# Who takes Sinkhorn's reciprocals: a power of -1 on GpSimd instead of a reciprocal on VectorE

## The chip, the cores and the metric

The kernel runs on one core of a Trainium2 chip. The metric is the device time of one execution in microseconds (us). The core has TensorE (PE) for matmuls, VectorE (DVE), ScalarE (ACT) and GpSimd (POOL) for everything elementwise, and SyncE (SP), which here only starts DMAs. Each engine takes its own instructions in the order in which they are written, and engines wait for each other by counting semaphores.

## The reference, cut to what matters

The input is x of shape 8 x 512 x 2048. A gated cross attention over windows of 128 columns comes first, and then a gated mixing block, which holds the loop that this case is about:

```python
x = x + jnp.tanh(g_xattn[0]) * xattn(_layernorm(x), ctx_4096, ...)
x = x + jnp.tanh(g_ffn[0]) * ffn(_layernorm(x), ...)

# inside ffn: 4 x 4 logits for each of the 8 * 512 rows
def sinkhorn_log(logits, num_iters=50, tau=0.1):
    Z = logits / tau
    def step(carry, _):
        u, v = carry
        u = -jax.nn.logsumexp(Z + v[..., None, :], axis=-1)
        v = -jax.nn.logsumexp(Z + u[..., :, None], axis=-2)
        return ((u, v), None)
    (u, v), _ = jax.lax.scan(step, (u0, v0), None, length=num_iters)
    return jnp.exp(Z + u[..., :, None] + v[..., None, :])
...
x_mixed = jnp.einsum('btij,btjc->btic', H_res, x_streams)   # H_res from sinkhorn_log
```

## The kernel before, in words

Partitions hold 128 of the 512 rows at a time, so one batch element is four row tiles (DT = 4). Attention is done in 32 chunks of 512 columns (4 for each batch element), each chunk in 8 units. All engines loop over the same counter `g`: one step of `g` is one unit of attention, plus whatever the tables at the top of the program place at that step for other chunks and for the mixing block of the batch element before. 32 steps are one batch element. There is no planner: the order on each engine is the order of the calls in its loop over `g`.

The kernel does Sinkhorn's iterations in the linear domain. For each batch element `ke` is [128, 4 tiles, 4, 4], 64 numbers in a partition. The first of the 50 iterations is done with logarithms, and so is a return to them after iteration 25 (`return_scales`); the other 49 iterations are done as 98 half iterations. A half iteration multiplies `ke` by the scales of the other side, sums rows or columns (16 sums in a partition) and inverts the sums:

- GpSimd, `scale` (L522 to L526): `kp = ke * sa` or `kp = ke * sv`, 128x64. It waits for `scale_made` and counts `kp_made`. In 96 of the 98 halves there is such a product (`SCALED`); two halves for each batch element sum `ke` itself.
- VectorE, `half_iteration` (L1125 to L1141): a `tensor_reduce` of `kp` into `ssum` (L1134, 128x16), and behind it, by way of a wait on its own semaphore (`cf.link`), a `reciprocal` of `ssum` into `sa` or `sv` (L1135), which counts `scale_made`.

The halves of one batch element are a chain: no half starts before the one in front of it. `SINK` puts two iterations, four halves, into a step: 12 steps, the step with iteration 25 alone, a step for the logarithms, and 12 steps again. `half_at(f, its, 0)` to `half_at(f, its, 3)` in VectorE's loop stand between the attention's maximum (L1002), the reads of projections (L982, L1019) and `divide` (L1010), the sums of the mixing block's output (`add_stream` L1179, `add_y` L1192, `make_xpre` L1167) and the statistics (L968, L1043). `scale_at(f, its, 0)` to `scale_at(f, its, 3)` in GpSimd's loop stand between its other work, which the tables place once for each of four row tiles in 8 steps: `norm_x` (L454) behind the first, `split_ctx` (L465) behind the second, `split_x` (L460) behind the third. Behind the fourth come GpSimd's own DMAs, `add_x` (L474) and `store` (L480), four in 8 steps.

After iteration 25, VectorE holds until the scales are there and then asks ScalarE for their logarithms (L1137, L1138). After iteration 50 it holds in the same way and makes the mixing coefficients (`coefficients`, L1148 to L1161).

## Time and profile before

| | us |
|---|---|
| median of 3 runs | 1913.92 |
| lowest and highest | 1908.95, 1915.57 |
| the profiled execution's own time | 1919.96 |
| its span, first to last instruction | 1918.2 |

| engine | busy us | share of the span | instructions |
|---|---|---|---|
| PE (matmul) | 1418.2 | 74% | 12448 |
| DVE | 1434.5 | 75% | 3684 |
| ACT | 942.4 | 49% | 1889 |
| POOL | 868.2 | 45% | 1461 |

The shares are means over a span with three kinds of stretches: about 340 us at the start without any Sinkhorn, some 1250 us in which attention of one batch element and the mixing block of the one before run side by side, and the last 300 us, in which only the mixing block is left and TensorE is mostly idle. How full an engine is where the change acts has to be read from a stretch, not from this table.

### The profile page before, as it was taken

The page shows a single profiled execution, that of the slowest core. Times are in us where ns is not written, and L with a number is a line of the kernel's source. Part 1 is how long each engine was busy: PE and PEld are TensorE (multiplying, and loading weights), DVE is VectorE, ACT ScalarE, POOL GpSimd, SP SyncE. Part 2 cuts the span into 40 slices and gives each one's busy share as a digit, 9 for nine tenths or more (in the row PEclk, how much of TensorE's full clock was granted, in tenths as well). Part 3 has the DMA queues.
Part 4 walks back from the last instruction along what each step waited for, and adds up shares of the span by engine and source line. Part 5 has one row for each costly group of instructions (what it writes and reads, how often), then busy time and mean ns, then how long its engine had stood idle before and what let it go on. Part 6 is the DMA issues. An engine that isn't in the chain of part 4 may idle for free. (4 is left out here: it accounts for less than half of the span.)

```text
span 1918.2 us, 35465 instructions
## 1 busy us (share of the span) xinstructions
PE 1418.2 (74%) x12448; PEld 857.5 (45%) x12448; DVE 1434.5 (75%) x3684; ACT 942.4 (49%) x1889; POOL 868.2 (45%) x1461
## 2 busy tenths in 40 slices
PE   2778899888888888888888888888888976421223
PEld 1545555544554455455544454445544554210111
DVE  3344445666688888888888888888888888777787
ACT  2445565555465556555655555554555554210112
POOL 4433333445445554555455645555565523323310
PEclk9889998999899999998999989998999986755656
DMA  7556655565566666666666656666555543321132
GB/s 247 150 152 198 177 159 150 156 165 152 151 177 189 188 189 176 176 184 167 183 192 188 184 170 177 185 173 168 167 168 168 144 119 92 88 77 44 55 101 107
DMA packets 173984, 299.79 MB, mean 156 GB/s; under 512 B 23664, under 2 KB 74736, under 8 KB 169712
## 3 DMA queue, kind: packets, MB, share of 16 engines
q1 hardware_dynamic: 147184, 230.41, 39.3%
q0 software_dynamic: 26624, 67.12, 15.2%
q8 instruction: 100, 1.64, 0.3%
q14 instruction: 76, 0.62, 0.1%
HBM read 179.75 MB, written 67.11 MB: 129 GB/s over the span
## 5 line engine op out<-in xcount | busy, mean ns | idle before, releaser
L526 POOL TENSOR_TENSOR kp<-ke,sv 128x64 f32<-128x64 f32 x376 | 186.5, 496 | 254.7 <-DVE sv L1135 245.0
L1134 DVE TENSOR_REDUCE ssum<-kp 128x16 f32<-128x64 f32 x768 | 181.9, 237 | 147.3 <-POOL kp L526 142.3
L604 PE MATMUL pr<-x_hl,wq 128*128 128x512 bf16 x768 | 234.1, 470 | 67.4 <-POOL x_hl L460 67.4
L526 POOL TENSOR_TENSOR kp<-ke,sa 128x64 f32<-128x64 f32 x392 | 126.7, 323 | 347.1 <-DVE sa L1135 347.1
L805 ACT ACTIVATE probs<-st_ps,key_bias 128x512 f32<-128x512 f32 x256 | 174.3, 681 | 184.1 <-PE st_ps L702 182.8
L1002 DVE TENSOR_REDUCE negm<-s_ps 128x4 bf16<-128x512 f32 x256 | 167.9, 656 | 111.9 <-PE s_ps L688 103.7
L631 PE MATMUL pr<-o_sb,wo 128*128 128x512 bf16 x768 | 186.2, 389 | 49.1 <-DVE o_sb L1026 38.1
L460 POOL TENSOR_TENSOR x_hl<-xc,x_hl 128x512 bf16<-128x512 f32 x128 | 172.6, 1349 | 103.4 <-ACT x_hl L773 103.4
L618 PE MATMUL pr<-wv,ctx_hl 128*128 128x256 bf16 x1536 | 193.1, 286 | 6.4 <-POOL ctx_hl L465 6.4
L465 POOL TENSOR_TENSOR ctx_hl<-ctx_raw,ctx_hl 128x512 bf16<-128x512 f32 x128 | 151.2, 1182 | 71.1 <-ACT ctx_hl L767 71.0
L604 PE MATMUL pr<-x_hl,wk 128*128 128x512 bf16 x768 | 176.4, 379 | 0.0
L604 PEld LDWEIGHTS pr<-x_hl,wq 128*128 128x128 bf16 x768 | 88.3, 118 | 193.1 <-issue 112.5
L651 PE MATMUL pr<-id_sb,x1c 128*128 128x128 f32 x512 | 89.9, 315 | 113.2 <-DMA x1c<-in_dram 113.2
L618 PEld LDWEIGHTS pr<-wv,ctx_hl 128*128 128x128 bf16 x1536 | 153.4, 103 | 40.7 <-issue 17.8
L700 PE MATMUL st_ps<-q_st,k_st 96*128 96x128 bf16 x1024 | 149.0, 222 | 17.9 <-ACT probs L805 14.8
L1010 DVE TENSOR_TENSOR o_sb<-av_ps,rden 128x128 f32<-128x128 f32 x256 | 70.5, 276 | 109.1 <-ACT rden L814 108.9
L787 ACT ACTIVATE q_hl<-pr,bq_sb 128x512 bf16<-128x512 f32 x64 | 44.0, 687 | 217.1 <-PE pr L604 217.1
L702 PE MATMUL st_ps<-id_bf,negm 128*128 128x128 bf16 x1024 | 148.4, 222 | 0.0
L675 PE MATMUL pr<-id_sb,xpre 128*128 128x128 f32 x128 | 24.5, 325 | 161.9 <-DVE xpre L1167 161.9
L631 PEld LDWEIGHTS pr<-o_sb,wo 128*128 128x128 bf16 x768 | 69.3, 99 | 167.4 <-issue 67.0
L728 PE MATMUL f<-wb,xpt 128*128 128x512 f32 x256 | 134.3, 674 | 8.5 <-ACT xpt L884 8.5
L1179 DVE SCALAR_TENSOR_TENSOR otile<-x1t_even,cmat,otile 128x512 f32<-128x512 f32 x192 | 136.0, 749 | 0.3
(140 smaller groups left out, 3106.8 us busy)
## 6 DMA issues: line engine op xcount, KB each, us to landing
xs<-in_dram SPq DMA_DIRECT2D x128, 256.0 KB, 3.8
xc<-in_dram SPq DMA_DIRECT2D x32, 1024.0 KB, 5.6
ctx_raw<-in_dram SPq DMA_DIRECT2D x32, 1024.0 KB, 5.2
x1c<-in_dram POOLq DMA_DIRECT2D x64, 512.0 KB, 6.0
x_dram<-x1c SPq DMA_DIRECT2D x32, 1024.0 KB, 5.4
out_dram<-otile POOLq DMA_DIRECT2D x64, 512.0 KB, 3.8
q_st<-q_hl SPq DMA_DIRECT2D x384, 64.0 KB
k_st<-k_hl SPq DMA_DIRECT2D x384, 64.0 KB
```

The lines of the kernel that those rows point to most:

```text
L460: nc.gpsimd.tensor_tensor(x_hl[:, G % 2, 1, t, :], xc[:, t, :], x_hl[:, G % 2, 0, t, :], ALU.subtract).then_inc(x_split, 1)
L465: ins = nc.gpsimd.tensor_tensor(ctx_hl[:, 1, t, :], ctx_raw[:, t, :], ctx_hl[:, 0, t, :], ALU.subtract)
L526: nc.gpsimd.tensor_tensor(kp[:], ke[:], v, ALU.mult).then_inc(kp_made, 1)
L604: ins = nc.tensor.matmul(bank(what)[:], w[:, a, t, i * P:(i + 1) * P], x_hl[:, G % 2, m, t, :], start=(t == 0 and a + m == 0), stop=(t == ...
L618: ins = nc.tensor.matmul(bank(what)[:, j * E:(j + 1) * E], ctx_hl[:, a, t, win], wv[:, m, t, :], start=(t == 0 and a + m == 0), stop=(t == ...
L631: ins = nc.tensor.matmul(bank(what)[:], wo[:, a, et, t * P:(t + 1) * P], o_part(G, et, m), start=(et == 0 and a + m == 0), stop=(et == ET ...
L700: nc.tensor.matmul(part, k_st[0:ROWS, G % 2, et, h, win], q_st[0:ROWS, G % 2, et, h, win], start=True, stop=False)
L702: ins = nc.tensor.matmul(part, negm[:, k % 2, h:h + 1].broadcast_to([P, P]), id_bf[:], start=False, stop=True)
L805: nc.scalar.activation(probs[:, k % 2, :], st_ps[:], ACT.Exp, bias=key_bias[:, b % 2, w:w + 1], scale=SCALE).then_inc(exp_done, 1)
L1002: nc.vector.tensor_reduce(negm[:, k % 2, :], s_ps[:].rearrange("p (h j) -> p h j", h=HPT), AX.X, ALU.max, negate=True).then_inc(max_done, 1)
L1134: cf.link(nc.vector.tensor_reduce(s_t, k, AX.X, ALU.add))
L1179: ins = nc.vector.scalar_tensor_tensor(out=otile[:, i, :], in0=x1[:, j * C:(j + 1) * C], scalar=cmat[:, f % 2, t, i, j:j + 1], in1=otile[: ...
```

## The change: GpSimd inverts the sums

A new function `invert` on GpSimd raises the 16 sums of each partition to the power of -1. It is a `tensor_tensor` with a tile `minus` that holds -1.0 everywhere. `scale` calls it in front of the product that needs its result. Two inversions have no product behind them (after iteration 25 and after iteration 50); `invert_last` does these, behind `scale_at(f, its, 3)`. VectorE keeps the sum and drops the reciprocal and the wait on its own semaphore. `sum_made` is the new semaphore from VectorE to GpSimd; `scale_made` is now counted by GpSimd; GpSimd's products and VectorE's waits at those two halves wait for it.

```diff
@@ -212,6 +212,7 @@
         gt = sb("gt", [P, 8])
         ones = sb("ones", [P, P])
         spare = sb("spare", [P, 1])
+        minus = sb("minus", [P, DT * N])
         csum = sb("csum", [P, NL])
         bn_a = sb("bn_a", [P, DT, 4, 6])
         mv_a = sb("mv_a", [P, DT, 2])
@@ -310,6 +311,7 @@
         x1_added = [sem(f"x1_added{i}") for i in range(2)]
         x1_stored = sem("x1_stored")
         x1t_loaded = [sem(f"x1t_loaded{i}") for i in range(2)]
+        sum_made = sem("sum_made")
         scale_made = sem("scale_made")
         kp_made = sem("kp_made")
         bias_ready = sem("bias_ready")
@@ -519,8 +521,15 @@
                     newton(r[:, 5, :], r[:, 2, :], r[:, 4, :], r[:, 1, :])
                     nc.gpsimd.tensor_tensor(r[:, 5, :], r[:, 5, :], r[:, 3, :], ALU.mult).then_inc(rb_ready, 1)
 
+            def invert(f, it, half):
+                n = HALVES * f + 2 * (it - 1) + half
+                pool.wait_ge(sum_made, n + 1)
+                dst = (sv if half else sa)[:].rearrange("p t i -> p (t i)")
+                nc.gpsimd.tensor_tensor(dst, ssum[:], minus[:], ALU.pow).then_inc(scale_made, 1)
+
             def scale(f, it, half):
 
+                invert(f, it if half else it - 1, 1 - half)
                 pool.wait_ge(scale_made, HALVES * f + 2 * (it - 1) + half)
                 v = bcast(sa[:], 3, N) if half else bcast(sv[:], 2, N)
                 nc.gpsimd.tensor_tensor(kp[:], ke[:], v, ALU.mult).then_inc(kp_made, 1)
@@ -530,8 +539,15 @@
                 if (it, half) in SCALED:
                     scale(f, it, half)
 
+            def invert_last(f, its):
+                if its[0] == RETURN:
+                    invert(f, RETURN, 1)
+                elif its[1] == ITERS - 1:
+                    invert(f, ITERS - 1, 1)
+
             pool.memset(q_st[ROWS:ROWS + 1], 1.0).then_inc(zeroed, 1)
             pool.wait_ge(zeroed, 1)
+            pool.memset(minus[:], -1.0)
             variance(0)
             xstat(0)
             for g in range(FIRST, LAST):
@@ -555,6 +571,7 @@
                 for H, t in at_step(g, -2, LOW_X_AT):
                     split_x(H, t)
                 scale_at(f, its, 3)
+                invert_last(f, its)
                 if 0 <= G - 1 < NG and r in (6, 7):
                     add_x(G - 1, r - 6)
                 for done, t in tiles_at(g, 4):
@@ -1131,8 +1148,7 @@
                     k = ke[:]
                 if half:
                     k = k.rearrange("p t i j -> p t j i")
-                cf.link(nc.vector.tensor_reduce(s_t, k, AX.X, ALU.add))
-                nc.vector.reciprocal((sv if half else sa)[:], s_t).then_inc(scale_made, 1)
+                nc.vector.tensor_reduce(s_t, k, AX.X, ALU.add).then_inc(sum_made, 1)
                 if half and it == RETURN:
                     dve.wait_ge(scale_made, HALVES * f + 2 * it)
                     ask(nc.vector.memset(spare[:, 0:1], 0.0))
```

GpSimd in program order, around the end of iteration 25 of the first batch element; `scale_made` before is counted by VectorE. Before:

```order
L526 TENSOR_TENSOR kp<-ke,sv 128x64 [waits scale_made]
L526 TENSOR_TENSOR kp<-ke,sa 128x64 [waits scale_made]
L465 TENSOR_TENSOR ctx_hl<-ctx_raw,ctx_hl 128x512 [waits ctx_hi]
L454 TENSOR_SCALAR xc<-xc,ra 128x512 [waits xstat_ready,xc_loaded]
L465 TENSOR_TENSOR ctx_hl<-ctx_raw,ctx_hl 128x512 [waits ctx_hi]
```

And the same place of the changed kernel (its lines 528, 535, 467 and 456 are `invert`, `scale`, `split_ctx` and `norm_x`):

```order
L528 TENSOR_TENSOR sv<-ssum,minus 128x16 [waits sum_made]
L535 TENSOR_TENSOR kp<-ke,sv 128x64 [waits scale_made]
L528 TENSOR_TENSOR sa<-ssum,minus 128x16 [waits sum_made]
L535 TENSOR_TENSOR kp<-ke,sa 128x64 [waits scale_made]
L467 TENSOR_TENSOR ctx_hl<-ctx_raw,ctx_hl 128x512 [waits ctx_hi]
L528 TENSOR_TENSOR sv<-ssum,minus 128x16 [waits sum_made]
L456 TENSOR_SCALAR xc<-xc,ra 128x512 [waits xstat_ready,xc_loaded]
```

Each product now has an inversion right in front of it, and the last inversion of iteration 25 stands behind the subtraction that splits the context.

VectorE in program order at the same place, before:

```order
L1134 TENSOR_REDUCE ssum<-kp 128x16 [waits kp_made]
L1135 RECIPROCAL sv<-ssum 128x16 [waits dve_ffn]
L1002 TENSOR_REDUCE negm<-s_ps 128x4 [waits st_full,s_full]
L1134 TENSOR_REDUCE ssum<-kp 128x16 [waits kp_made]
L1135 RECIPROCAL sa<-ssum 128x16 [waits dve_ffn]
L982 SCALAR_TENSOR_TENSOR q_hl<-pr,bq_sb,q_hl 128x512 [waits qk_hi]
L1010 TENSOR_TENSOR o_sb<-av_ps,rden 128x128 [waits rden_done]
L1134 TENSOR_REDUCE ssum<-kp 128x16 [waits kp_made]
L1135 RECIPROCAL sv<-ssum 128x16 [waits dve_ffn]
L1138 MEMSET spare 128x1 [waits scale_made]
L1002 TENSOR_REDUCE negm<-s_ps 128x4 [waits st_full,s_full]
```

And of the changed kernel (its lines 1151, 1154, 1019, 999 and 1027 are the sum, the request to ScalarE, the maximum, a read of a projection and `divide`):

```order
L1151 TENSOR_REDUCE ssum<-kp 128x16 [waits kp_made]
L1019 TENSOR_REDUCE negm<-s_ps 128x4 [waits st_full,s_full]
L1151 TENSOR_REDUCE ssum<-kp 128x16 [waits kp_made]
L999 SCALAR_TENSOR_TENSOR q_hl<-pr,bq_sb,q_hl 128x512 [waits qk_hi]
L1027 TENSOR_TENSOR o_sb<-av_ps,rden 128x128 [waits rden_done]
L1151 TENSOR_REDUCE ssum<-kp 128x16 [waits kp_made]
L1154 MEMSET spare 128x1 [waits scale_made]
L1019 TENSOR_REDUCE negm<-s_ps 128x4 [waits st_full,s_full]
```

The reciprocals are gone from VectorE and nothing else there changes place. Its wait at L1154 is now one for GpSimd.

## Rows read from the trace of the kernel before

**Rows 1.** The page: the chain that ended last, its shares by engine

```profile
DVE 7%; POOL 1%; DMA 1%; issue 1%; PE 0%; ACT 0%; DVEq 0%; ACTq 0%
```

**Rows 2.** Busy us of each engine by stretch (start:end, length, then engines)

```profile
1039.90:1089.90 50.00, 41.02 (x380) 24.48 (x380) 44.68 (x119) 30.15 (x60) 29.39 (x50) 0.95 0.63 186
1744.00:1918.00 174.00, 44.81 (x77) 18.89 (x75) 129.62 (x294) 27.36 (x41) 35.92 (x89) 0.60 0.23 82
```

**Rows 3.** Waits: who waited for whom, us in total, times, longest

```profile
POOL kp L526 <- DVE sa L1135: 347.1, 269, 9.9
POOL kp L526 <- DVE sv L1135: 245.0, 273, 2.6
...
DVE ssum L1134 <- POOL kp L526: 142.3, 293, 1.9
```

**Rows 4.** Groups by line: busy us, mean ns of one, idle before

```profile
L1134 DVE TENSOR_REDUCE ssum<-kp 128x16 f32<-128x64 f32 x768 | 181.9, 237 | 147.3 <-POOL kp L526 142.3
...
L1135 DVE RECIPROCAL sa<-ssum 128x16 f32<-128x16 f32 x392 | 99.2, 253 | 13.4
L1135 DVE RECIPROCAL sv<-ssum 128x16 f32<-128x16 f32 x392 | 99.2, 253 | 13.4
```

**Rows 5.** The same view: GpSimd's products and its other instructions

```profile
L526 POOL TENSOR_TENSOR kp<-ke,sv 128x64 f32<-128x64 f32 x376 | 186.5, 496 | 254.7 <-DVE sv L1135 245.0 <-ACT x_hl L773 8.4
L460 POOL TENSOR_TENSOR x_hl<-xc,x_hl 128x512 bf16<-128x512 f32 x128 | 172.6, 1349 | 103.4 <-ACT x_hl L773 103.4
L526 POOL TENSOR_TENSOR kp<-ke,sa 128x64 f32<-128x64 f32 x392 | 126.7, 323 | 347.1 <-DVE sa L1135 347.1
L487 POOL TENSOR_TENSOR rb<-rb 128x4 f32<-128x4 f32 x16 | 3.2, 203 | 1.3
```

**Rows 6.** GpSimd in order of time, last batch element: start, us, instruction, idle before

```profile
1749.35 0.30 POOL L526 TENSOR_TENSOR kp<-ke,sv 128x64 f32<-128x64 f32 x1 [0.66 <-DVE sv L1135]
1750.27 0.30 POOL L526 TENSOR_TENSOR kp<-ke,sa 128x64 f32<-128x64 f32 x1 [0.62 <-DVE sa L1135]
```

**Rows 7.** VectorE over the same moments

```profile
1749.69 0.22 DVE L1134 TENSOR_REDUCE ssum<-kp 128x16 f32<-128x64 f32 x1 [0.41 <-POOL kp L526]
1749.94 0.25 DVE L1135 RECIPROCAL sa<-ssum 128x16 f32<-128x16 f32 x1
1750.60 0.26 DVE L1134 TENSOR_REDUCE ssum<-kp 128x16 f32<-128x64 f32 x1 [0.41 <-POOL kp L526]
```

**Rows 8.** GpSimd in order of time: a chain of its own; a DMA between products

```profile
1057.06 1.25 POOL L474 DMA_DIRECT2D x1c<-in_dram  x1
1057.88 0.77 POOL L526 TENSOR_TENSOR kp<-ke,sv 128x64 f32<-128x64 f32 x1
...
1103.39 0.20 POOL L487 TENSOR_TENSOR rb<-rb 128x4 f32<-128x4 f32 x1
1103.68 0.20 POOL L488 TENSOR_SCALAR rb<-rb 128x4 f32<-128x4 f32 x1
```

**Rows 9.** Both engines where iteration 25 ends

```profile
1021.82 1.16 POOL L465 TENSOR_TENSOR ctx_hl<-ctx_raw,ctx_hl 128x512 bf16<-128x512 f32 x1
...
1022.18 0.25 DVE L1134 TENSOR_REDUCE ssum<-kp 128x16 f32<-128x64 f32 x1
1022.46 0.25 DVE L1135 RECIPROCAL sv<-ssum 128x16 f32<-128x16 f32 x1
```

**Rows 10.** VectorE in order of time: two of the 32 stretches between sums

```profile
1048.48 1.36 DVE L1179 SCALAR_TENSOR_TENSOR otile<-x1t_even,cmat,otile 128x512 f32<-128x512 f32 x2
1049.88 0.22 DVE L1134 TENSOR_REDUCE ssum<-kp 128x16 f32<-128x64 f32 x1
1050.13 0.25 DVE L1135 RECIPROCAL sa<-ssum 128x16 f32<-128x16 f32 x1
1051.15 0.27 DVE L1134 TENSOR_REDUCE ssum<-kp 128x16 f32<-128x64 f32 x1 [0.77 <-POOL kp L526]
```

## The prediction, made before the changed kernel ran

> **What bounds the kernel now.** I read the chain that ended last first, and put it aside: its shares add up to about a tenth of the span [rows 1], so it says little of the stretches in which the change acts. Next the busy time by stretch. Between 1039.9 and 1089.9 us stand exactly 8 steps with four half iterations each, 32 halves in 50 us, 6.25 us a step. VectorE is busy for 44.7 of these 50 us, TensorE for 41.0, GpSimd for 29.4 [rows 2]. VectorE is the fullest, and GpSimd has 20.6 us to spare.
>
> Then the waits, to see whether that spare time is free. It is not all free: GpSimd waits 592 us in total for the two reciprocals, and VectorE waits 142 us for GpSimd's product [rows 3]. The halves are one chain that goes to and fro between the two engines. Where VectorE has nothing else to do between two halves, the chain turns as fast as it can: a product every 0.92 to 0.96 us, of which GpSimd works 0.30 and sits idle 0.62 to 0.66 [rows 6], while VectorE sums for 0.22 to 0.26, inverts for 0.25 and then waits 0.41 [rows 7]. Where VectorE has other work between two halves, that work covers GpSimd's part: behind the 1.36 us of L1179 the sum starts at once, without a wait [rows 10]. So a step is VectorE's own work plus a few bare turns of the chain, and what counts on GpSimd is how much longer its part of a half may get before that cover is gone.
>
> **What the change removes.** 784 reciprocals of 0.253 us on VectorE, 198 us [rows 4], or 8.1 us of each 50, with some 0.03 us of a wait on its own semaphore at each. Nothing else of VectorE moves.
>
> **What it adds.** 784 powers of 16 elements on GpSimd, P us each, and one more handoff inside GpSimd, from the power to the product. That handoff is a wait on its own semaphore. Its price is in the trace: chained GpSimd instructions of 0.20 us stand 0.29 us apart, so 0.09 us [rows 8]. The handoffs from VectorE to GpSimd and back stay as they were. A memset of 16 elements at the start is nothing beside the wait for the first statistics. The power also reads two operands in SBUF like the product does, so the slower products that show up in the mean (0.496 us for those from sv, 0.323 for those from sa, [rows 5]) may change places with it; I leave their sum alone.
>
> **The price P.** No instruction before is a power. From below it can hardly be less than the product of the same form: that takes 0.203 us for 4 elements and 0.30 us for 64 [rows 5, 6], so 0.0016 us an element over 0.197, and 0.22 us for 16. [...] Taking 30 to 50 such steps (my assumption, no row shows it) and for each the 0.0016 us an element of a small product gives 16 x 30 x 0.0016 + 0.2 = 1.0 us to 16 x 50 x 0.0016 + 0.2 = 1.5 us. With the 0.0023 us an element of the large subtractions ((1.349 - 0.2) / 512, [rows 5]) 50 steps are 2.0 us. I take 1.0 us, the lower figure of the nearer row, because a step inside one instruction has no load and store of its own; the ends that I keep are 0.22 and 2.0.
>
> The Trainium skill has no price for a power. Its "GPSIMD Engine Reference", section "Performance pitfalls for Q7 kernels", says that a chain of dependent fp32 operations costs 4 cycles an element for each link, and its table puts the engine at 1.2 GHz. No run here shows it yet. By it 30 links over 16 elements would be 1.6 us and 0.2 over, 1.8 us, an estimate from that page; that is the second rival below.
>
> **The sum.** With P near 1 us the cover is gone and GpSimd sets the pace, so I count its 8 steps. Its busy time is 29.4 us [rows 2], less 0.9 us, since two of the DMAs that it issues in 8 steps are shown as 1.25 us while the next product starts 0.82 us after them [rows 8]: 28.5 us. Behind 16 of the 32 products stand other instructions in its order (the four each of L454, L465 and L460, and four DMAs), so that VectorE's sum is done beside them; there only the handoff of 0.09 us is idle, 1.4 us. Behind the other 16 it waits for the sum: the idle 0.64 us of a bare turn [rows 6], less the reciprocal and its wait (0.25 and 0.03), plus the handoff of 0.09, is 0.45 us, 7.2 us in all. 28.5 + 1.4 + 7.2 = 37.1, so 8 steps take 37 + 32 P us, as long as that is clearly over what VectorE needs. For P = 1.0 this is 69 us where there were 50, and a step is 8.6 us. VectorE's work without the reciprocals, 36.6 us, fits into that; only the few stretches of over 1.5 us between two sums make GpSimd wait, which I leave out with about 1 us.
>
> There are 784 / 32 = 24.5 such groups of 32 halves in the program: 24.5 x 19 = 466 us. The last batch element, in which TensorE is nearly idle [rows 2], runs the same chain (rows 6 are from there) and loses as much. At the end of iteration 25 VectorE now holds the whole queue behind L1154 until GpSimd has finished the subtraction in front of the last power. That subtraction runs from 1021.8 to 1023.0, and the sum is ready at 1022.4 [rows 9]: 0.6 us more beside the power itself, and at iteration 50 nothing more than the power. What is queued there are the attention's maximum and the read of a projection, for which TensorE and ScalarE wait. 8 x 0.6 and the two handoffs are some 8 us. Together 1918 + 466 + 8 = 2392 us of span, 2394 of execution. The profiled execution was 1919.96, 6 us over the median of 1913.92, so for a median I say **2390 us**. In general the time is about 1608 + 784 P for P over 0.4.
>
> **Rival 1: the power is as cheap as a product, and the change is faster.** For it speaks that VectorE is the fullest engine and loses 8.1 of its 44.7 us. With P = 0.22 the bare turn stays what it was: 0.25 + 0.03 leave, 0.22 + 0.09 come. Of 32 stretches between sums, 18 have over 0.8 us of other work on VectorE and can be shorter by 0.28 us each, 5 us in 50; where GpSimd's own 1.2 to 1.6 us stand in front of the power (12 of 32) the power is late and takes about half of that back. That leaves 2.5 to 5 us in 50, or 60 to 120 us: 1800 to 1855 us. This is the other side, and it decides at P of about 0.33 us, where the two effects meet. [...]
>
> **Rival 2: GpSimd computes the power link by link.** P = 1.4 to 2.0 us, by the larger of the figures above. At 1.8 us it is 1608 + 1411 = 3020 us. [...]
>
> **Rival 3: the power costs about twice the reciprocal.** The Trainium skill says in "GPSIMD Engine Reference", section "Engine selection", that elementwise work is about half as fast here as on VectorE. From rows, twice 0.253 us is P = 0.5: 37 + 16 = 53 us for 8 steps plus about 1 us in which VectorE is late, 24.5 x 4 = 98 us more, or about 2010 us. Rows 4 and 5 put a small product on GpSimd (0.22) level with a small operation on VectorE, so the rule is weak for small tiles.
>
> **Rival 4: nothing to see.** P between 0.30 and 0.36 us, gains and losses equal, 1908 to 1920.
>
> **How the numbers follow.** 2390 us, with P between 0.7 and 1.4 and so 2150 to 2700: chance 0.40. Rival 2, 2700 to 3180: 0.22. Rival 3, P from 0.36 to 0.7, 1920 to 2150: 0.19. Rival 1, under 1908: 0.12. Rival 4: 0.04. The last 0.03 are for a power that is not computed in the engine's vector form at all and takes ten times as long. This measurement can tell a change from none at about 0.3%, 6 us. Slower by more: 0.40 + 0.22 + 0.19 + 0.03 = 0.84; within: 0.04; faster: 0.12. The range that holds 8 in 10 must reach to both sides, since the price is open by a factor of nine: 1850 to 3100 leaves out the better half of rival 1 and the upper end of rival 2, about 0.2.
>
> **What would show it.** In the profile after, the group of L528 gives P directly, and the rest hangs on it. If I am right, its mean is near 1 us, GpSimd is the fullest engine with about 80% of the span (868 + 784 = 1652 us), 8 steps take 69 us, VectorE's waits at L1151 for L535 grow from 142 to over 500 us, and all of VectorE's, ScalarE's and TensorE's busy times stay as they were apart from the reciprocals. TensorE will wait more and its granted clock may fall below the 0.95 of these steps [rows 2]; that would lengthen its work, but not the end, as long as GpSimd sets the pace. The sum is wrong if 8 steps do not take 37 + 32 P with the measured P. The direction is wrong if P is under 0.33 us.

## The result: twice the time, far outside the range

| | median us | lowest to highest | executions |
|---|---|---|---|
| before | 1911.85 | 1908.95 to 1915.57 | 4 |
| after | 3855.24 | 3854.09 to 3859.77 | 4 |

The ratio is 2.0145, with a 95% interval of 2.0091 to 2.0199. The forecast was 2390 us and the range ended at 3100 us. The direction was right and the size was not. The page of the changed kernel begins with the engines' busy time; the second line below is the share of the chain that ended last, the third the granted clock in 40 slices, in tenths.

```profile
PE 1727.5 (45%) x12293; PEld 1015.1 (26%) x12448; DVE 1330.7 (35%) x2900; ACT 962.6 (25%) x1889; POOL 3135.6 (81%) x2246
...
POOL 8%; DVE 2%; issue 1%; DMA 1%; PE 0%; ACT 0%; DVEq 0%; ACTq 0%
...
PEclk9998666766777666686668666676667655555556
```

GpSimd went from 868 to 3136 us and is now the fullest engine. VectorE's busy time fell by 104 us, not by the 198 us of its reciprocals; ScalarE's rose by 20. TensorE's is 309 us longer for the same matmuls, since its granted clock is lower: 0.691 as a mean where it was 0.876 (1.0 is its upper level of 2.4 GHz, 0.5 the lower one of 1.2 GHz). This is a consequence of the waiting: TensorE is busy for 45% of the span, and VectorE's wait for its scores (L1019, L1002 before) even fell, from 103.7 to 79.6 us. The groups answer to [rows 4, 5], with busy us, mean ns of one, then the idle time before and who ended it:

```profile
L528 POOL TENSOR_TENSOR sv<-ssum,minus 128x16 f32<-128x16 f32 x392 | 1224.3, 3123 | 90.0 <-DVE ssum L1151 88.9
L528 POOL TENSOR_TENSOR sa<-ssum,minus 128x16 f32<-128x16 f32 x392 | 1148.5, 2930 | 151.6 <-DVE ssum L1151 151.6
L1151 DVE TENSOR_REDUCE ssum<-kp 128x16 f32<-128x64 f32 x768 | 186.1, 242 | 2232.6 <-POOL kp L535 2232.6
...
L535 POOL TENSOR_TENSOR kp<-ke,sa 128x64 f32<-128x64 f32 x392 | 117.3, 299 | 30.7
L535 POOL TENSOR_TENSOR kp<-ke,sv 128x64 f32<-128x64 f32 x376 | 112.4, 299 | 29.5
...
L1195 DVE SCALAR_TENSOR_TENSOR otile<-x1t_even,cmat,otile 128x512 f32<-128x512 f32 x192 | 156.8, 857 | 0.3
```

The power takes 3.03 us as a mean over its 784. With that alone GpSimd has 2373 us more to do. VectorE's wait for the product, which answers to the last line of [rows 3], went from 142 to 2233 us. The products, read in [rows 5] as 496 and 323 ns, are now all 299 ns. The last row is part of the answer to VectorE's missing gain: this group, L1179 before, took 136.0 us with 749 ns each, and takes 857 now. Two instructions of the chain in order of time, first on GpSimd and then on VectorE, show what [rows 6, 7] showed of before:

```profile
2001.00 2.90 POOL L528 TENSOR_TENSOR sv<-ssum,minus 128x16 f32<-128x16 f32 x1 [0.44 <-DVE ssum L1151]
2003.98 0.30 POOL L535 TENSOR_TENSOR kp<-ke,sv 128x64 f32<-128x64 f32 x1
2004.26 0.77 POOL L456 TENSOR_SCALAR xc<-xc,ra 128x512 f32<-128x512 f32 x1
2005.00 2.90 POOL L528 TENSOR_TENSOR sa<-ssum,minus 128x16 f32<-128x16 f32 x1
```

```profile
2000.66 0.26 DVE L1151 TENSOR_REDUCE ssum<-kp 128x16 f32<-128x64 f32 x1 [2.27 <-POOL kp L535]
2000.84 0.68 DVE L1019 TENSOR_REDUCE negm<-s_ps 128x4 bf16<-128x512 f32 x1
2004.31 0.22 DVE L1151 TENSOR_REDUCE ssum<-kp 128x16 f32<-128x64 f32 x1 [2.79 <-POOL kp L535]
```

GpSimd goes from the power to the product 0.08 us later; where another instruction of its own stands behind the product, the next power needs no wait at all. VectorE does its 0.68 us of other work and then stands for 2.79 us. A half turns in 3.65 us here, where a bare one (with no other work on either engine) took 0.92. The stretch of 8 steps answers to the first line of [rows 2], with the columns as there:

```profile
1723.50:1853.80 130.30, 57.27 (x375) 32.88 (x380) 42.08 (x86) 29.82 (x55) 121.48 (x81) 0.68 0.25 71
```

It took 50.0 us and takes 130.3. GpSimd is busy for 121.5 of them and idle for 8.8. ScalarE's 29.8 us are nearly the 30.2 of before.

### The profile page after: what moved, and what is told of

Its sections match the earlier page's. It is cut to its first block and busy times, and to the rows that moved or that the text cites. A ratio compares the mean times of both kernels' runs of the same rounds, so it can differ in the third digit from the quotient of the medians.

```text
span 3852.6 us, 35310 instructions
## 1 busy us (share of the span) xinstructions
PE 1727.5 (45%) x12293; PEld 1015.1 (26%) x12448; DVE 1330.7 (35%) x2900; ACT 962.6 (25%) x1889; POOL 3135.6 (81%) x2246
## 5 line engine op out<-in xcount | busy, mean ns | idle before, releaser
L528 POOL TENSOR_TENSOR sv<-ssum,minus 128x16 f32<-128x16 f32 x392 | 1224.3, 3123 | 90.0 <-DVE ssum L1151 88.9
L528 POOL TENSOR_TENSOR sa<-ssum,minus 128x16 f32<-128x16 f32 x392 | 1148.5, 2930 | 151.6 <-DVE ssum L1151 151.6
L705 PE MATMUL s_ps<-k_st,q_st 97*128 97x128 bf16 x1024 | 127.2, 262 | 641.1 <-DVE negm L1019 629.4
L648 PE MATMUL pr<-o_sb,wo 128*128 128x512 bf16 x706 | 248.5, 499 | 350.1 <-DVE x1c L1036 140.3
L732 PE MATMUL av_ps<-probs,v_t 128*32 128x128 f32 x2048 | 137.9, 350 | 335.8 <-DVE o_sb L1027 335.6
L705 PEld LDWEIGHTS s_ps<-k_st,q_st 97*128 97x128 bf16 x1024 | 87.2, 116 | 732.4 <-DVE negm L1019 484.3
L635 PE MATMUL pr<-wv,ctx_hl 128*128 128x256 bf16 x1536 | 232.2, 322 | 7.1 <-POOL ctx_hl L467 6.9
L621 PE MATMUL pr<-x_hl,wk 128*128 128x512 bf16 x736 | 206.6, 439 | 4.3 <-issue 2.9
L1019 DVE TENSOR_REDUCE negm<-s_ps 128x4 bf16<-128x512 f32 x256 | 174.3, 681 | 84.3 <-PE s_ps L705 79.6
L717 PE MATMUL st_ps<-q_st,k_st 96*128 96x128 bf16 x1024 | 192.4, 264 | 16.9 <-DVE negm L1019 9.4
L719 PE MATMUL st_ps<-id_bf,negm 128*128 128x128 bf16 x1024 | 191.8, 263 | 0.0
L1195 DVE SCALAR_TENSOR_TENSOR otile<-x1t_even,cmat,otile 128x512 f32<-128x512 f32 x192 | 156.8, 857 | 0.3
```

The source lines that it names most:

```text
L528: nc.gpsimd.tensor_tensor(dst, ssum[:], minus[:], ALU.pow).then_inc(scale_made, 1)
L621: ins = nc.tensor.matmul(bank(what)[:], w[:, a, t, i * P:(i + 1) * P], x_hl[:, G % 2, m, t, :], start=(t == 0 and a + m == 0), stop=(t == ...
L635: ins = nc.tensor.matmul(bank(what)[:, j * E:(j + 1) * E], ctx_hl[:, a, t, win], wv[:, m, t, :], start=(t == 0 and a + m == 0), stop=(t == ...
L648: ins = nc.tensor.matmul(bank(what)[:], wo[:, a, et, t * P:(t + 1) * P], o_part(G, et, m), start=(et == 0 and a + m == 0), stop=(et == ET ...
L705: ins = nc.tensor.matmul(s_ps[:, h * W:(h + 1) * W], q_st[0:ROWS + 1, G % 2, et, h, win], k_st[0:ROWS + 1, G % 2, et, h, win], start=True, ...
L717: nc.tensor.matmul(part, k_st[0:ROWS, G % 2, et, h, win], q_st[0:ROWS, G % 2, et, h, win], start=True, stop=False)
```

## The experiments

Eleven kernels, in three groups; the kernel before ran beside each group, with medians of 1913.66, 1912.88 and 1912.17 us. Two questions were open. Why does the power cost 2.9 us, and does the sum hold with its real price? And would the change have been faster had the power been cheap, as Rival 1 said?

### probe: powers by themselves

The kernel before, with a chain of GpSimd instructions ahead of its loop, on tiles that nothing else uses.

```diff
+            cp.link(nc.gpsimd.tensor_tensor(po[:, 0:16], pb[:, 0:16], pe_[:, 0:16], ALU.mult))
+            cp.link(nc.gpsimd.tensor_tensor(po[:, 0:1], pb[:, 0:1], pe_[:, 0:1], ALU.pow))
+            ... (0:4, 0:16, 0:64, 16 partitions x 16, then exponents 2 and -0.5 and a base of 1, at 0:16)
```

> The kernel before, with a row of GpSimd instructions of its own ahead of the loop, each waiting for the one before, on tiles that nothing else uses: one product of 128x16, powers of -1 of 128x1, 128x4, 128x16, 128x64 and 16x16 (16 partitions), powers of 2 and of -0.5 of 128x16 with base 2.7, and a power of -0.5 with base 1. The time stays within 10 us of the kernel before. Theory A (the power has this price by itself, element by element): 128x16 takes 2.90 us here too, where VectorE does nothing with two operands, and 128x1, x4 and x64 take 0.37, 0.87 and 11.0 us (0.2 and 0.169 an element); 16 partitions cost what 128 do. Theory C (the power is slow only beside VectorE, which shares memory access with GpSimd): 128x16 takes about 1 us here. A price that depends on exponent or base would show in the last three.

The single execution took 1926.2 us, 12.5 more than before, a little over the 10 that were expected for the delayed start. GpSimd in order of time (L541 is a product, L542 to L546 are powers of -1, L548 has the exponent 2, the last row below a base of 1):

```profile
8.15 0.21 POOL L541 TENSOR_TENSOR pout<-pbase,pexp 128x16 f32<-128x16 f32 x1
8.44 0.58 POOL L542 TENSOR_TENSOR pout<-pbase,pexp 128x1 f32<-128x1 f32 x1
9.10 1.02 POOL L543 TENSOR_TENSOR pout<-pbase,pexp 128x4 f32<-128x4 f32 x1
10.20 2.90 POOL L544 TENSOR_TENSOR pout<-pbase,pexp 128x16 f32<-128x16 f32 x1
13.18 10.55 POOL L545 TENSOR_TENSOR pout<-pbase,pexp 128x64 f32<-128x64 f32 x1
23.80 2.89 POOL L546 TENSOR_TENSOR pout<-pbase,pexp 16x16 f32<-16x16 f32 x1
...
26.98 2.90 POOL L548 TENSOR_TENSOR pout<-pbase,pexp 128x16 f32<-128x16 f32 x1
...
33.36 2.90 POOL L552 TENSOR_TENSOR pout<-pbase,pexp 128x16 f32<-128x16 f32 x1
```

From 16 to 64 elements the price rises by 7.65 us for 48 elements, 0.159 us an element; 2.90 less 16 x 0.159 leaves 0.36 us, and the rows of 1 and 4 elements put the fixed part at 0.42 to 0.38. The exponents, the two bases and the number of partitions change nothing. So the price belongs to the operation and its length, not to its place in the kernel, and Theory C falls: VectorE is idle beside the last row. A product of the same form is 0.21 us.

### cheap: the same instruction as a product

The power becomes a product of ones with ones, so the sums aren't inverted and the scales are 1. Instructions, operand shapes and waits stay.

```diff
-                nc.gpsimd.tensor_tensor(dst, ssum[:], minus[:], ALU.pow).then_inc(scale_made, 1)
+                nc.gpsimd.tensor_tensor(dst, minus[:], minus[:], ALU.mult).then_inc(scale_made, 1)
```

> The changed kernel with a product of two constant tiles of ones (128x16) in the place of each power, so the reciprocal is left out and every scale is 1; waits and order are those of the change. Theory A (the price P alone decides): P is 0.22 us, and by rival 1 of the prediction the kernel is faster than before, 1800 to 1855 us, 8 steps in 45 to 47.5 us. Theory B (the inversion costs by where it stands: one more handoff in the chain and the place behind GpSimd's other work): no gain, 1905 us or more.

1925.83 us (1920.46 to 1928.44), ratio 1.0057 [1.0041, 1.0073]: 0.6% slower than before, though VectorE's busy time is 1305.3 us instead of 1434.5. The bare turn is as long as it was (0.92 to 0.96 us between these powers' stand-ins, L528):

```profile
1751.05 0.21 POOL L528 TENSOR_TENSOR sv<-minus 128x16 f32<-128x16 f32 x1 [0.38 <-DVE ssum L1151]
1751.97 0.21 POOL L528 TENSOR_TENSOR sa<-minus 128x16 f32<-128x16 f32 x1 [0.33 <-DVE ssum L1151]
1752.93 0.65 POOL L528 TENSOR_TENSOR sv<-minus 128x16 f32<-128x16 f32 x1 [0.37 <-DVE ssum L1151]
```

The third row is the other finding: the same instruction takes 0.65 us when VectorE runs an operation with two operands in SBUF beside it. Between 400 and 1900 us, 133 stand-ins run beside L1195, which reads two tiles in SBUF, and their median is 0.65 us; 84 run beside the maximum L1019, which reads PSUM, and take 0.21. VectorE and GpSimd over one stretch between two sums:

```profile
980.82 0.27 DVE L1151 TENSOR_REDUCE ssum<-kp 128x16 f32<-128x64 f32 x1 [0.23 <-POOL kp L535]
981.01 2.11 DVE L1195 SCALAR_TENSOR_TENSOR otile<-x1t_even,cmat,otile 128x512 f32<-128x512 f32 x2
983.38 0.22 DVE L1151 TENSOR_REDUCE ssum<-kp 128x16 f32<-128x64 f32 x1 [0.26 <-POOL kp L535]
...
981.87 0.66 POOL L528 TENSOR_TENSOR sv<-minus 128x16 f32<-128x16 f32 x1
...
982.61 0.67 POOL L535 TENSOR_TENSOR kp<-ke,sv 128x64 f32<-128x64 f32 x1
```

From sum to sum this is 2.56 us. The same stretch of the kernel before takes 2.16 us, with the reciprocal in it:

```profile
978.11 0.25 DVE L1134 TENSOR_REDUCE ssum<-kp 128x16 f32<-128x64 f32 x1
978.39 0.25 DVE L1135 RECIPROCAL sv<-ssum 128x16 f32<-128x16 f32 x1
978.56 1.67 DVE L1179 SCALAR_TENSOR_TENSOR otile<-x1t_even,cmat,otile 128x512 f32<-128x512 f32 x2
980.27 0.22 DVE L1134 TENSOR_REDUCE ssum<-kp 128x16 f32<-128x64 f32 x1
```

Rival 1 falls as it was priced: with an instruction that takes its 0.22 us alone there is no gain. In its place it takes 0.43 us for sv and 0.24 for sa as a mean. VectorE's wait for the product is 309.7 us in total where it was 142.3 [rows 3].

### four: a power of 4 of the 16 elements

The other 12 scales are set to 1 once.

```diff
-                nc.gpsimd.tensor_tensor(dst, ssum[:], minus[:], ALU.pow).then_inc(scale_made, 1)
+                nc.gpsimd.tensor_tensor(dst[:, 0:4], ssum[:, 0:4], minus[:, 0:4], ALU.pow).then_inc(scale_made, 1)
```

> The changed kernel with powers of 4 of the 16 sums (128x4); the other 12 scales stay 1, so three quarters of the inversions are left out. Theory A: P about 0.87 us, 1608 + 784 x 0.87 = 2290 us. If the power has a large fixed part (call, table, setup) and a small one for each element, P stays near 2.5 us and the time over 3400.

2391.86 us in a single execution. The power took 1.13 us as a mean (1.229 for sv, 1.035 for sa), not the expected 0.87, and 8 steps took 70.5 us:

```profile
1409.71:1480.25 70.54, 48.70 (x382) 27.25 (x381) 41.92 (x87) 29.11 (x55) 61.30 (x81) 0.83 0.45 131
```

By chance its time is the forecast one: the prediction's own formula says 1608 + 784 x 1.132 = 2495 us for this price. The powers take 36.9 us of this stretch, so GpSimd is busy for 24.4 us outside them; in the changed kernel it is 121.5 - 97.5 = 24.0 us.

### half: GpSimd inverts one side alone

`sa` stays with GpSimd's power, `sv` goes back to VectorE's reciprocal.

```diff
-                nc.vector.tensor_reduce(s_t, k, AX.X, ALU.add).then_inc(sum_made, 1)
+                if half:
+                    cf.link(nc.vector.tensor_reduce(s_t, k, AX.X, ALU.add))
+                    nc.vector.reciprocal(sv[:], s_t).then_inc(sv_made, 1)
+                else:
+                    nc.vector.tensor_reduce(s_t, k, AX.X, ALU.add).then_inc(sum_made, 1)
```

> Half of the change: row sums are inverted by GpSimd's power (sa, 392 powers), column sums by VectorE's reciprocal (sv, 392) as before. Theory A: 8 steps take GpSimd 28.5 us of old work less 2 for products that meet less of VectorE, 16 x 2.93 = 47 us of powers and about 12 us of handoffs and of waits for VectorE, 85 us in all, so 1918 + 24.5 x 35 = 2775 us. If the loss came from a queue that is full only when every half has its power, half of the powers would cost clearly less than half: under 2500 us.

2864.15 us in a single execution, 950 over before for 392 powers of 2.93 us: 2.42 us for each. The whole change is 1943 us for 784, 2.48 us for each. The cost goes by the number of powers, and the side that was tested costs about as much as the mean of both. My 2775 was 3% low.

### none: no inversion at all

The product waits for the sum itself; the scales are 1.

```diff
-                nc.gpsimd.tensor_tensor(dst, ssum[:], minus[:], ALU.pow).then_inc(scale_made, 1)
...
-                pool.wait_ge(scale_made, HALVES * f + 2 * (it - 1) + half)
```

> No inversion on any engine (left out; every scale is 1): VectorE sums, GpSimd multiplies, and the product waits for the sum itself. It differs from the run with the cheap product only by that 0.21 us instruction and its handoff. Theory D (the 198 us that VectorE loses are worth much, and the run with the cheap product gave them back because a GpSimd instruction and a handoff stand in the chain, and because it meets VectorE's two-operand instructions): a bare turn falls from 0.93 to 0.96 us to about 0.65, and about three quarters of 32 x 0.28 us in 8 steps come back, 1918 - 24.5 x 6.7 = 1755 us. Theory E (VectorE's time is not what these steps are made of, so nothing is won by emptying it): 1900 us or more.

1823.78 us, ratio 0.9526 [0.9499, 0.9552]: between what the two theories said. The bare turn fell to 0.63 to 0.67 us:

```profile
1701.74 0.30 POOL L532 TENSOR_TENSOR kp<-ke,sa 128x64 f32<-128x64 f32 x1 [0.76 <-DVE ssum L1150]
1702.41 0.30 POOL L532 TENSOR_TENSOR kp<-ke,sv 128x64 f32<-128x64 f32 x1 [0.38 <-DVE ssum L1150]
1703.04 0.30 POOL L532 TENSOR_TENSOR kp<-ke,sa 128x64 f32<-128x64 f32 x1 [0.33 <-DVE ssum L1150]
```

So 90 us is what the inversion costs where it stands in the kernel before. Two things left together: the reciprocal's place in the turn, and 153 us of VectorE's busy time (1281.4 instead of 1434.5). The cheap stand-in uses all of the 90 us and 12 us more.

### one_operand: the stand-in reads one tile

```diff
-                nc.gpsimd.tensor_tensor(dst, ssum[:], minus[:], ALU.pow).then_inc(scale_made, 1)
+                nc.gpsimd.tensor_scalar(dst, minus[:], 1.0, None, ALU.mult).then_inc(scale_made, 1)
```

> The run with the cheap product once more, with a GpSimd instruction of one operand (a tensor_scalar, 128x16) in the place of the product of two; the inversion is left out. If reading a second operand is what makes GpSimd's small instruction and VectorE's L1195 slow each other (0.67 us for 0.21, 0.82 for 0.75), this instruction keeps about 0.21 us, L1195 goes back to about 0.75 us and the time is 1900 us or less. If it is the position in the chain alone, the time is that of the cheap product, 1926 us, within 6.

1950.15 us, ratio 1.0182 [1.0158, 1.0205], which neither theory expected. The instruction takes 0.25 us by itself, 0.04 more than the product with two operands, and the bare turn is 0.98 to 1.02 us. Beside VectorE it is stretched like the product: its mean for sv is 466 ns, and VectorE's L1195 takes 819 ns as in cheap (749 in the kernel before). So GpSimd's second operand isn't what makes the two engines slow each other. The means of both sides are 0.036 us above cheap's, 29 us in all, and the bare turn is 0.06 us longer, which would be 47 us if every turn were bare; the time rose by 24.

### three: three chained products in place of the power

```diff
+                cp.link(nc.gpsimd.tensor_tensor(spare3[:], minus[:], minus[:], ALU.mult))
+                cp.link(nc.gpsimd.tensor_tensor(spare3[:], spare3[:], minus[:], ALU.mult))
+                nc.gpsimd.tensor_tensor(dst, spare3[:], minus[:], ALU.mult).then_inc(scale_made, 1)
```

> Three chained products of 128x16 in the place of each power (reciprocal left out, scales 1). P is 3 x 0.22 + 2 x 0.09 = 0.84 us, up to 0.95 where they meet VectorE. The prediction's sum with the measured relief of the products (8 steps in 33 + 32 P) says 1505 + 784 P, 2165 to 2250 us; the uncorrected sum, 1608 + 784 P, 2267 to 2350. Theory that the power as an instruction does more harm than its length: under 2100.

2302.65 us in a single execution. The three products and the handoffs between them add up to 802 us, 1.02 us a half, above the 0.84 to 0.95 expected. It is the same slope as the powers', by instructions that have nothing of a power: what counts is the length of the chain on GpSimd.

### twice: more work for VectorE, outside the chain

The kernel before, with a second reciprocal of ones behind each.

```diff
+                nc.vector.reciprocal(again[:].rearrange("p t i -> p (t i)"), ones[:, 0:16])
```

> The kernel before with a second reciprocal of 128x16 on VectorE behind each of the 784, of a constant tile, into a tile that nothing reads: 198 us more on VectorE, none of it in the chain. Theory D (VectorE sets the pace except in bare turns, where 0.25 us more hide in its wait of 0.41): about two thirds of it show, 2045 us. Theory E: under 1945 us.

1939.47 us, ratio 1.0128 [1.0099, 1.0157]:

```profile
L1137 DVE RECIPROCAL again<-ones 128x16 f32<-128x16 f32 x784 | 152.7, 195 | 0.0
```

VectorE's busy time, in which overlapping records count once, rose by only 73 us, from 1434.5 to 1507.6, though the records of the second reciprocal add up to 152.7. The reason stands in the order of time:

```profile
1049.50 0.25 DVE L1136 RECIPROCAL sa<-ssum 128x16 f32<-128x16 f32 x1
1049.67 0.20 DVE L1137 RECIPROCAL again<-ones 128x16 f32<-128x16 f32 x1
1049.78 1.31 DVE L1020 SCALAR_TENSOR_TENSOR x1c<-pr,bo_sb,maskbc 128x512 f32<-128x512 f32 x2
```

Its record overlaps both neighbours, and what follows it starts 0.11 us behind it. So 73 us more of VectorE cost 26 us, about a third. VectorE is the fullest engine of the kernel before, and yet most of the work that the next half doesn't wait for is hidden: its wait for the product fell from 142.3 to 106.7 us.

### beside: the stand-in, but outside the chain

As none, with a product of ones into a tile that nobody reads, issued before the wait for the sum.

```diff
+                nc.gpsimd.tensor_tensor(junk[:, n % 4], minus[:], minus[:], ALU.mult).then_inc(scale_made, 1)
-                nc.gpsimd.tensor_tensor(dst, ssum[:], minus[:], ALU.pow).then_inc(scale_made, 1)
```

> The run without any inversion, with the product of ones (128x16) back on GpSimd 784 times, but out of the chain: it stands ahead of GpSimd's wait for the sum and writes a tile that nothing reads (inversion left out). It tells apart why the cheap product in the chain cost 102 us over none (1926 against 1824). Theory F (length of the chain: 0.21 us and a handoff of 0.08 in every turn): GpSimd does it while it waits, and the time is that of none, 1824 to 1840 us. Theory G (two engines that read and write SBUF at once slow each other, so each GpSimd instruction costs wherever it stands): 1880 to 1926 us.

1838.43 us, ratio 0.9613 [0.959, 0.9636]. The same 784 instructions cost 102 us inside the chain (cheap against none) and 15 us beside it, where they run while VectorE sums:

```profile
1701.81 0.21 POOL L528 TENSOR_TENSOR junk<-minus 128x16 f32<-128x16 f32 x1
...
1702.22 0.30 POOL L537 TENSOR_TENSOR kp<-ke,sv 128x64 f32<-128x64 f32 x1 [0.20 <-DVE ssum L1156]
```

The row of their group answers Theory G:

```profile
L528 POOL TENSOR_TENSOR junk<-minus 128x16 f32<-128x16 f32 x784 | 260.8, 345 | 1.3 <-DVE ssum L1156 0.4
```

These products are stretched as they were in cheap (345 ns as a mean, 336 there), and the time is almost that of none. What cheap has besides is 26 us more of VectorE's busy time (1305.3 against 1279.4), since its operations are stretched too; that is far less than the 87 us between the two kernels.

### shortest: the least that stands in GpSimd's place

A memset of one element in place of the power; the scales are 1.

```diff
-                nc.gpsimd.tensor_tensor(dst, ssum[:], minus[:], ALU.pow).then_inc(scale_made, 1)
+                pool.memset((sv if half else sa)[:, 0, 0:1], 1.0).then_inc(scale_made, 1)
```

> The changed kernel with the shortest GpSimd instruction that I have, a memset of one element in each partition, in the place of the power (inversion left out, scales 1). About 0.06 to 0.1 us and the handoff of 0.08 stand in the chain. Theory F: the turn is 0.15 to 0.18 us longer than with none where it was 0.30 longer with the cheap product, so about half of the 102 us, 1865 to 1885 us. If the handoff alone made the cost, it is near 1926.

1861.6 us, ratio 0.9718 [0.9691, 0.9745], slightly under what was expected. The memset takes 0.10 us as a mean for sa and 0.15 for sv. Beside L1194 it is not stretched, 0.10 us in all of the 133 cases between 400 and 1850 us; the mean for sv comes from 40 memsets of 0.6 us, which all stand directly behind GpSimd's own DMA of L475, as in the first two rows. The bare turn is 0.79 to 0.84 us (the last two):

```profile
401.46 1.22 POOL L475 DMA_DIRECT2D x1c<-in_dram  x1 [0.18 <-issue]
402.25 0.55 POOL L526 MEMSET sv<- 128x1 f32 x1
...
1701.38 0.10 POOL L526 MEMSET sv<- 128x1 f32 x1 [0.36 <-DVE ssum L1150]
...
1702.17 0.10 POOL L526 MEMSET sa<- 128x1 f32 x1 [0.31 <-DVE ssum L1150]
```

### own: the opposite move

If the length of the chain is what counts, the product belongs to VectorE wherever VectorE waits for it. The kernel before, with 287 of its 768 products moved there: those halves at which the trace shows VectorE waiting for 0.15 us or more, in a table by batch element. It computes everything.

```diff
+                    if (f, it, half) in OWN:
+                        dve.wait_ge(scale_made, HALVES * f + 2 * (it - 1) + half)
+                        v = over_j(sa[:]) if half else over_i(sv[:])
+                        cf.link(nc.vector.tensor_tensor(kp[:], ke[:], v, ALU.mult))
```

> A version that computes the reference, out of what the runs say: the chain's length counts, and more work on VectorE costs little (153 us more of it made 26 us). The kernel before, with the product of 287 of the 768 halves moved from GpSimd to VectorE, those at which VectorE waited 0.15 us or more for GpSimd's product in the trace of before. Each such wait (158 us in all, 0.54 us each) is replaced by a product of 0.225 us and a wait on its own semaphore of 0.03. Theory F: up to 158 - 287 x 0.26 = 83 us less, and since some waits will move to the next halves, 1850 to 1880 us. Rival: VectorE is full in the steps beside attention, and what the waits give is taken by 287 x 0.26 = 74 us of work that is now late for TensorE and ScalarE: 1905 us or more.

1881.83 us (1878.61 to 1891.1), ratio 0.9843 [0.9817, 0.9869]: 1.6% faster than the kernel before, just outside the expected 1850 to 1880 us, and the fastest of the kernels that leave nothing out. The bare turn without a handoff between engines is 0.80 to 0.85 us:

```profile
1701.32 0.26 DVE L1149 TENSOR_REDUCE ssum<-kp 128x16 f32<-128x64 f32 x1
1701.62 0.25 DVE L1150 RECIPROCAL sv<-ssum 128x16 f32<-128x16 f32 x1
1701.91 0.23 DVE L1140 TENSOR_TENSOR kp<-ke,sv 128x64 f32<-128x64 f32 x1
1702.17 0.22 DVE L1149 TENSOR_REDUCE ssum<-kp 128x16 f32<-128x64 f32 x1
```

VectorE's wait for GpSimd's product fell from 142 to 2.7 us, and its busy time rose from 1434.5 to 1504.9. In the two profiled executions, 140 us of this wait went away and VectorE worked 70 us more; the span fell by 41 us, from 1918.2 to 1876.8. The other 28 us are new idle time of VectorE, 15 of them in its wait for ScalarE at `divide` (108.9 to 123.7 us).

## Why the prediction was wrong

**The step that failed is "The price P".** It took 1.0 us for a power of 16 elements, from an assumption, 30 to 50 arithmetic steps, times 0.0016 us an element of a small product. The 0.0016 was a row; the number of steps was none, and no run shows it either. What the runs show in its place is the whole: 2.90 us for 16 elements, with 0.159 us an element, as much as 100 such products, and 0.4 us fixed instead of 0.2. The upper end of 2.0 us was too low as well: it was built of the same assumption with another price for a step, so 3100 us was too low for the range. Three rivals made the power cheaper than the middle and one dearer, up to 2.0 us; for all that lay above 2.0 us there was one line with a chance of 0.03. The row of 4 elements in probe would have been enough to settle it: 1.02 us for a quarter of the elements.

**The rule of the Trainium skill** that was Rival 2's came nearer. In "GPSIMD Engine Reference", section "Performance pitfalls for Q7 kernels", a link of a dependent fp32 chain costs 4 cycles an element. The measured 0.159 us an element would be 48 links by it, an estimate from that page with its clock of 1.2 GHz; no run here shows how many links there are. My 30 links in Rival 2 gave 1.8 us, 0.62 of what was measured. The rule of Rival 3, elementwise work at half of VectorE's speed, doesn't cover a power: 2.90 us stand against 0.253 for VectorE's reciprocal [rows 4], a factor of 11. For a small product it is too high: 128x64 takes 0.30 us on GpSimd, and own shows it with 0.23 on VectorE, a factor of 1.3.

**The sum was nearly right.** With the measured price it gives 1608 + 784 x 3.027 = 3981 us, 3% over the 3855. Of 8 steps it said 37.1 us without the powers, of which 8.6 idle. Measured are 130.3 us less the 97.5 that the powers take in this stretch, 32.8 us, of which 8.8 idle. The 4.2 us are as much as the products lost: 13.7 us in 8 steps before, 9.6 after. "I leave their sum alone" was wrong. Beside VectorE's operations with two operands in SBUF a product took 0.66 us before (L1179), beside its reads of PSUM 0.30, and VectorE is now done with the former long before the product starts; so all of them take 0.30 us. With 32.8 + 32 P in 8 steps, and 24.5 x 4.2 = 103 us less in all, the time is 1505 + 784 P, and this holds over a factor of three in P and for two kinds of instruction:

| | P, us | 1505 + 784 P | measured |
|---|---|---|---|
| three (products) | 1.023 | 2307 | 2303 |
| four (powers of 4) | 1.132 | 2392 | 2392 |
| after (powers of 16) | 3.027 | 3878 | 3855 |

The constant was read from a stretch of the changed kernel; the two smaller kernels, one execution each, test it.

**The mechanism was right.** GpSimd sets the pace (81% of the span; the prediction's "about 80%" was a slip, since its 1652 us of 2392 are 69%, which is what four shows), VectorE waits at the sum for the product, and ScalarE's work in 8 steps is unchanged. TensorE's clock fell, in the 8 steps from 0.95 to 0.68, and lengthened its work by 16 us in a stretch of 130. That this did not touch the end is argued, not tested: the sum, which has no term for it, is met.

At the end of iteration 50 VectorE holds 8 times for 3.0 us, the power alone, as said. At the end of iteration 25 it was shown waiting for the last power once, for 3.7 us, where 0.6 us and a power were said for each of the 8; mostly it still had other work then. "All of VectorE's busy times stay" was wrong: 1434.5 - 198 = 1236 us were said and 1331 measured. Of the 95 us, 45 are there in none too (1281), where no instruction took the reciprocal's place: records of VectorE overlap where one instruction follows another at once (in cheap's last rows L1179 starts 0.17 us behind a reciprocal of 0.25), so 784 fewer of them take less than their sum from the busy time. And 36 are in the two groups of L1179, 269.5 us before, 277.7 in none and 305.2 now, when they run beside the power. That GpSimd's idle time in 8 steps is nearly the one forecast, 8.8 against 8.6 us, speaks against a cost of it.

**Rival 1 erred in what a cheap power would bring.** By the means in the kernel, shortest (0.12 us) is 2.8% faster and cheap (0.33) 0.6% slower; on the line between them the break-even is at 0.30 us, close to the 0.33 that was said. But the rival put the power at 0.22 us there, and the instruction that takes 0.21 alone takes 0.33, since it is stretched to 0.65 in just the stretches where VectorE has much to do, and holds VectorE up in turn. The gain was counted from VectorE's load, 18 stretches shorter by 0.28 us each, 60 to 120 us in all, and none, with nothing in the reciprocal's place, gains 90 us. What the rival had wrong was the charge against it: the stand-in costs 102 us over none. beside shows where that comes from: the same instructions, stretched as much, cost 102 us in the chain and 15 us next to it. How the 90 us split isn't shown. If VectorE's load counts at the rate of twice, 26 us for 73, the 153 us less of it would be worth 54 us, an estimate, and the shorter turn the rest.

## What to carry to other kernels

An operation that no trace shows is the whole prediction when it stands in a dependent chain: measure it alone, at two lengths, before anything is moved, and if that can't be done keep the upper bound open by a factor and not by a half. In a chain that goes to and fro between two engines the length of a turn comes first. Here length added to it cost from a quarter of itself (shortest: 38 us over none for 784 times 0.20 us, memset and handoff) to all of it, where GpSimd set the pace (three, four and the change). GpSimd's work beside the chain cost 15 of its 188 us. The load of the fullest engine isn't free either: VectorE's 73 us cost 26. own shows which of the two weighs more here: VectorE was 70 us fuller, the turn shorter, and the kernel 30 us faster. So look at the turn first, whether a handoff can be taken out or a link given to the engine that is faster at it, and then at the loads.

## What the runs showed of the hardware

- A power on GpSimd, fp32: 0.58, 1.02, 2.90 and 10.55 us for 1, 4, 16 and 64 elements in a partition, and for 16 elements 2.9 us whatever the exponent (-1, 2, -0.5), the base (2.7 or 1) and the number of partitions (16 or 128). An exponent of 2 is no cheaper.
- Small GpSimd instructions are stretched two- to threefold, from 0.21 to 0.65 us and from 0.30 to 0.67, while VectorE runs an operation with two operands in SBUF, and not beside its maximum, which reads PSUM (0.21 and 0.30 beside L1019). VectorE's operation (L1195, 128x512) takes 819 ns as a mean in cheap and 857 beside the power, 762 in none. A GpSimd instruction with one operand is stretched as well (0.25 to 0.68 in one_operand); a memset, which reads nothing, is not (0.10 in shortest). The power itself is hardly stretched: 3.03 against 2.90.
- Directly behind GpSimd's DMA for x1c its next small instruction shows up longer: a memset of 0.10 us with 0.55 in shortest, a product of 0.30 with 0.77 [rows 8].
- A second reciprocal of 128x16 behind the first delays what follows on VectorE by 0.11 us, though its record is 0.195 long (twice).
- A `tensor_scalar` of 128x16 on GpSimd takes 0.25 us, longer than the product of two tiles with 0.21. A memset of one element takes 0.10.
- The mean granted clock of TensorE fell with the pace of the whole kernel: 0.95, 0.83 and 0.68 in 8 steps of 50, 71 and 130 us.
